# A new order for the prologue of two LoRA layers: x1, x2 and layer 1's rows loaded in front of A, three places for transposed x, and the table ends stored and gathered by themselves

## The reference

```python
# layer 0
result = jnp.einsum('bsd,od->bso', x, base_weight) + base_bias
h = jnp.einsum('bsd,brd->bsr', x, lora_A_w[ids0])
x = x + result + jnp.einsum('bsr,bor->bso', h, lora_B_w[ids0])
# layer 1
Bx = jnp.einsum('bni,bri->bnr', x, B[ids1])
x = x + jnp.einsum('bnr,bor->bno', Bx, A[ids1])   # scaling is 1
```

## Time and profile before

| | |
|---|---|
| time, median of 3 runs | 98.22 us (97.95 to 98.42) |
| the profiled execution | 97.92 us |
| its span, first to last instruction | 95.8 us |
| busy: PE, DVE, ACT, POOL | 91.5, 64.8, 58.7, 58.0 us |
| moved by DMA | 19.45 MB |
| mean granted clock of TensorE | 0.997 |

### The profile page before, as it was taken

One profiled execution on the slowest core, in us unless ns is written; L12 is line 12 of the kernel. 1 busy time (PEld: TensorE's weight loads), 2 busy tenths in 40 slices (PEclk: granted clock), 3 DMA queues, 4 the chain that ended last, 5 costly groups with the idle time before them and its releaser, 6 DMA issues.

```text
span 95.8 us, 2305 instructions
## 1 busy us (share of the span) xinstructions
PE 91.5 (96%) x662; PEld 90.0 (94%) x662; DVE 64.8 (68%) x120; ACT 58.7 (61%) x189; POOL 58.0 (61%) x126
## 2 busy tenths in 40 slices
PE   5999999999999999999999999999999999999980
PEld 5899999999899998999999999999999999999970
DVE  4499799227076468959587877768595868786460
ACT  0074598874588796748494948567584949480210
POOL 6504008850568999999576584959585766808500
PEclk9999999999999999999999999999999999999998
DMA  2999998968896289989996499992836354520205
GB/s 40 312 347 387 374 403 262 281 156 214 215 224 223 53 250 238 310 249 235 203 290 218 70 319 209 238 269 91 228 44 229 34 213 54 200 110 0 110 0 219
DMA packets 16335, 19.45 MB, mean 203 GB/s; under 512 B 1444, under 2 KB 11556, under 8 KB 16164
## 3 DMA queue, kind: packets, MB, share of 16 engines
q1 hardware_dynamic: 15040, 14.04, 50.1%
q0 software_dynamic: 1280, 5.28, 22.1%
q10 hardware_dynamic: 4, 0.00, 0.0%
HBM read 13.47 MB, written 5.84 MB: 202 GB/s over the span
## 4 chain that ended last, share of the span: by engine, by line
PE 90%; DVE 4%; ACT 2%; issue 1%; DVEq 0%; ACTq 0%
PE psum L394 55%; PE psum L440 11%; PE psum L432 4%; PE psum L362 4%; PE psum L480 4%; PE psum L378 4%; PE psum L370 3%; DVE table_rounded L640 3%; PE psum L466 2%; PE psum L414 1%; PE psum L405 1%; PE psum L448 1%; DVE y L679 1%; ACT row_ends L558 1%; ACT table_rounded L558 1%
## 5 line engine op out<-in xcount | busy, mean ns | idle before, releaser
L394 PE MATMUL psum<-wd,xt 128*128 128x256 f32 (+1 forms) x384 | 62.3, 310 | 0.0
L394 PEld LDWEIGHTS psum<-wd,xt 128*128 128x128 f32 x384 | 56.1, 188 | 0.0
L558 ACT ACTIVATE wd<-table_rounded 128x128 fp32r x128 | 27.7, 297 | 14.7 <-PE psum L394 12.5
L339 POOL TENSOR_TENSOR up_rows<-gathered_rows,up_rows 128x512 fp32r<-128x512 f32 x16 | 20.6, 1289 | 14.0 <-ACT up_rows L558 14.0
L322 POOL DMA_INDIRECT gathered_rows<-by_rank,rows x16 | 15.9, 996 | 6.3 <-DMA by_rank<-row_ends 3.8
L640 DVE TENSOR_TENSOR xt<-psum,xt 128x512 fp32r<-128x512 f32 x16 | 11.1, 691 | 6.6 <-ACT xt L558 5.9
L647 DVE STREAM_TRANSPOSE psum<-x_squares 128x512 f32<-128x512 f32 x13 | 14.4, 1110 | 0.0
L440 PE MATMUL psum<-up_rows,u_sel 128*128 128x256 f32 x96 | 14.2, 284 | 0.0
L440 PEld LDWEIGHTS psum<-up_rows,u_sel 128*128 128x128 f32 x96 | 12.8, 190 | 0.2
L659 DVE STREAM_TRANSPOSE psum<-psum 128x128 f32<-128x128 f32 x16 | 5.3, 330 | 11.2 <-PE psum L394 7.8
L332 POOL TENSOR_TENSOR g_sel<-gathered_rows,batch_mask 128x16 f32<-128x16 f32 x64 | 12.1, 227 | 0.9 <-DMA gathered_rows<-by_rank,rows 0.7
(11 more groups left out here) (60 smaller groups left out, 72.1 us busy)
## 6 DMA issues: line engine op xcount, KB each, us to landing
out<-y SPq DMA_DIRECT2D x15, 256.0 KB
x_squares<-in_x SPq DMA_DIRECT2D x8, 256.0 KB
w_rows<-in_L_cond_base_weight SPq DMA_DIRECT2D x4, 256.0 KB, 4.0
bw_rows<-in_L_cond_lora_B_w SPq DMA_DIRECT2D x1, 1024.0 KB, 7.0
a_rows<-in_L_cond_lora_A_w SPq DMA_DIRECT2D x1, 1024.0 KB, 9.2
by_rank<-bw_by_rank SPq DMA_DIRECT2D x4, 256.0 KB
x_squares<-in_x SPq DMA_DIRECT2D x8, 128.0 KB
x_rows<-in_x SPq DMA_DIRECT2D x3, 256.0 KB, 9.3
```

Of the source, the lines that this page charges most:

```text
L339: nc.gpsimd.tensor_tensor(out=up_rows[:, k % 2, LO, :], in0=gathered_rows[:, k % GATHERS, 0:D], in1=up_rows[:, k % 2, HI, :], op=ALU.subtr ...
L394: last = nc.tensor.matmul(bank_of(k, half)[:, start:end], xt[:, k % 2, c, x_part, :], wd[:, w_part, c, col:col + end - start], start=(c == ...
L558: return nc.scalar.activation(dst, src, ACT.Copy)
```

## The change

- **Loads.** SP loads x1 and x2 directly behind Bw, then A1's rows, the ids and the bias, and A last of all.
- **Start.** One warm-up product less, the two fillers gone; the copy of b1's columns moves from VectorE to ScalarE, which calls its table early.
- **xt** has three places. x2 is transposed and split before G, and base(2)'s left half is multiplied in front of D; base(0)'s right half is then one piece with D, and the separate `down` products go. up(0) stands one chunk (three products) before base(2)'s end, not two.
- **The table.** A row begins with its end (G, bias, padding: 148 numbers are stored) and is 660 numbers long instead of 644. The ends are stored in front of A1's rows, with a semaphore of their own. POOL gathers block 0's ends by themselves (a row is five units of 132 numbers), then waits for the rows; own_u(0) and g_select(0) read the small gather, and POOL issues all four gathers before g_select(1).
- **Block 0's low rows** are made on VectorE instead of POOL, and own_u(0) goes before x_turn(3). On ScalarE up_high(0) goes behind xt_high(3) and u_high(0), and a select reads its adapters before it waits.
- SP waits for gather 0 before it issues x's group 4.

```diff
--- before.py
+++ after.py
...
 SLOTS = 3
-WARM_UPS = 6
-FILLERS = 2
+X_SLOTS = 3
+WARM_UPS = 5
...
 GROUPS = (N0 + N1) * R // P
-G_COL, BB_COL = D, D + P
-ROW = BB_COL + 4
+G_COL, BB_COL = 0, P
+ENDS = P + 4
+UNITS = 5
+ROW = UNITS * ENDS
+UP_AT = ROW - D
...
 gathered_rows = sb("gathered_rows", [P, GATHERS, ROW])
-xt = sb("xt", [P, 2, C, 2, P], F32R)
+first_ends = sb("first_ends", [P, ENDS])
+xt = sb("xt", [P, X_SLOTS, C, 2, P], F32R)
...
+def ends(k, col, width):
+    if k == 0:
+        return first_ends[:, bass.ds(col, width)]
+    return gathered_rows[:, k % GATHERS, bass.ds(col, width)]
+def wait_ends(engine, k):
+    if k == 0:
+        engine.wait_ge(first_ends_gathered, 16)
+    else:
+        engine.wait_ge(gathered[k % GATHERS], 16 * (k // GATHERS) + 16)
+def wait_up_rows(engine, k):
+    if k == 0:
+        engine.wait_ge(first_up_ready, 1)
+    else:
+        engine.wait_ge(up_ready, k)
...
 def store_by_rank(queue, by_rank_part, n, row, c):
-    view = by_rank_dram[row:row + n * R, c * P:(c + 1) * P].rearrange("(n r) o -> n r o", r=R)
+    view = by_rank_dram[row:row + n * R, UP_AT + c * P:UP_AT + (c + 1) * P].rearrange("(n r) o -> n r o", r=R)
...
     sp.dma_start(bw_rows[:, :, :], lora_b.rearrange("n (c p) r -> (n c) p r", p=P)).then_inc(bw_in, 16)
-    sp.dma_start(a_rows[:, :, :], lora_a.rearrange("(g n) r d -> (n r) g d", g=C)).then_inc(a_in, 16)
     load_x(1)
+    load_x(2)
...
                  l1_a.rearrange("n (c p) r -> (n c) p r", p=P)).then_inc(a1_in, 16)
-    load_x(2)
...
     sp.dma_start(bias_all[:, :], bias.rearrange("(a n) -> a n", a=1).to_broadcast([P, D])).then_inc(bias_in, 16)
+    sp.dma_start(a_rows[:, :, :], lora_a.rearrange("(g n) r d -> (n r) g d", g=C)).then_inc(a_in, 16)
...
         store_by_rank(sp, bw_by_rank, N0, 0, c)
+    sp.wait_ge(zeros_ready, 2)
+    sp.wait_ge(bias_b1_ready, 1)
+    wait_drained(sp, "g")
+    sp.dma_start(by_rank_dram.rearrange("(g p) c -> p g c", p=P)[:, :, 0:UP_AT], row_ends[:, :, :]).then_inc(ends_stored, 16)
...
         store_by_rank(sp, a1_by_rank, N1, N0 * R, c)
-    sp.wait_ge(zeros_ready, 2)
-    sp.wait_ge(bias_b1_ready, 1)
-    wait_drained(sp, "g")
-    sp.dma_start(by_rank_dram.rearrange("(g p) c -> p g c", p=P)[:, :, D:ROW], row_ends[:, :, :]).then_inc(table_stored, 16)
...
     for k in range(NBLK - 1):
+        if k == 0:
+            sp.wait_ge(gathered[0], 16)
...
     nc.gpsimd.tensor_copy(rows[:, :], row_sums[:, :]).then_inc(rows_ready, 1)
+    nc.gpsimd.tensor_scalar(out=first_units[:, :], in0=row_sums[:, 0:1], scalar1=float(UNITS), scalar2=None,
+                            op0=ALU.mult).then_inc(rows_ready, 1)
...
         n1 = adapters_of(pool, k, L1)
-        pool.wait_ge(gathered[k % GATHERS], 16 * (k // GATHERS) + 16)
+        wait_ends(pool, k)
...
             last = nc.gpsimd.tensor_tensor(
-                out=g_sel[:, k % 2, b, L1, :], in0=gathered_rows[:, k % GATHERS, bass.ds(n1[b] * R + G_COL, R)],
+                out=g_sel[:, k % 2, b, L1, :], in0=ends(k, n1[b] * R + G_COL, R),
...
-    pool.wait_ge(rows_ready, 1)
+    pool.wait_ge(rows_ready, 2)
...
     pool.wait_ge(masks_ready, 4)
-    pool.wait_ge(table_stored, (2 * C + 1) * 16)
+    pool.wait_ge(ends_stored, 16)
+    nc.gpsimd.indirect_dma_start(out=first_ends[:, :], out_offset=None,
+                                 in_=by_rank_dram.rearrange("n (u c) -> (n u) c", c=ENDS),
+                                 in_offset=bass.IndirectOffsetOnAxis(ap=first_units[:, 0:1], axis=0),
+                                 ).then_inc(first_ends_gathered, 16)
+    pool.wait_ge(table_stored, 2 * C * 16)
...
     gather(1)
+    g_select(0)
     gather(2)
-    for k in range(NBLK):
+    gather(3)
+    for k in range(1, NBLK):
...
-    def base(k, chunks, with_d=True, halves=range(2), group_check=True):
+    def base(k, chunks, halves=range(2)):
...
-    def down(k, chunks):
-        half, at = U_AT[k % 2]
-        for c in chunks:
-            for x_part, d_part in HALVES:
-                nc.tensor.matmul(bank_of(k, half)[:, at:at + P], xt[:, k % 2, c, x_part, :],
-                                 wd[:, d_part, c, D_AT[k % 2]:D_AT[k % 2] + P],
-                                 start=False, stop=True, skip_group_check=True)
...
     w_fill(0)
-    keep_warm(FILLERS)
...
     base(0, range(C), halves=[0])
+    x_fill(2)
...
     base(1, range(C), halves=[1])
-    x_fill(2)
+    wait_x(2)
+    wait_drained(pe, "a0")
+    base(2, range(C), halves=[0])
...
     wait_drained(pe, "c1")
-    base(0, [0, 1], halves=[1], with_d=False, group_check=False)
     wait_d(0)
-    down(0, [0, 1])
-    base(0, [2, 3], halves=[1], group_check=False)
+    base(0, range(C), halves=[1])
...
-    wait_x(2)
-    base(2, range(C), halves=[0])
...
     wait_d(2)
-    base(2, [0, 1], halves=[1])
+    base(2, range(0, C - 1), halves=[1])
     up(0)
-    base(2, [2, 3], halves=[1])
+    base(2, [C - 1], halves=[1])
...
         act.wait_ge(xt_filled, k + 1)
+        if k >= X_SLOTS:
+            act.wait_ge(u_filled, k - X_SLOTS + 1)
+        copy(xt[:, k % X_SLOTS, :, HI, :], chunked(XT)).then_inc(xt_hi_ready, 1)
+    def select(k, layer, n=None):
+        ready, table = ((sel0_ready, table0_rounded), (sel1_ready, table1_rounded))[layer]
+        n = n or adapters_of(act, k, layer)
...
             act.wait_ge(u_filled, k - 1)
-        copy(xt[:, k % 2, :, HI, :], chunked(XT)).then_inc(xt_hi_ready, 1)
-    def select(k, layer, n=None):
-        ready, table = ((sel0_ready, table0_rounded), (sel1_ready, table1_rounded))[layer]
-        if k >= 2:
-            act.wait_ge(u_filled, k - 1)
-        n = n or adapters_of(act, k, layer)
...
+    act.wait_ge(warm_ready, 1)
+    copy(table_call[:, :], warm[:, 0:1])
+    wait_filled(act, "b1")
+    copy(b1_cols[:, :, :], chunked(fill_of("b1"))).then_inc(act_drained, 1)
+    w_high(0)
...
     first = {(k, layer): adapters_of(act, k, layer) for k in range(2) for layer in (L0, L1)}
-    for oc in range(C):
+    for oc in range(1, C):
...
     copy(a1_by_rank[:, 0:R // 2, :], a1_rows[:, :, 0:R // 2].rearrange("p o r -> p r o")).then_inc(a1_by_rank_ready, 1)
+    xt_high(2)
...
     select(1, L0, first[1, L0])
-    xt_high(2)
...
     select(2, L1)
-    up_high(0)
...
     u_high(0)
+    up_high(0)
...
     plus(0)
-    wait_filled(dve, "b1")
-    nc.vector.tensor_copy(b1_cols[:, :, :], chunked(fill_of("b1"))).then_inc(dve_drained, 1)
...
     xt_low(0)
-    for q in range(4):
+    def lay_bw(q):
...
+    for q in range(3):
+        lay_bw(q)
+    xt_low(1)
+    lay_bw(3)
...
     low(table1_rounded[:, :, LO, :, :], c1_by_adapter(), table1_rounded[:, :, HI, :, :]).then_inc(dve_drained, 1)
-    xt_low(1)
...
                             op0=ALU.mult).then_inc(ids_f_ready, 1)
+    xt_low(2)
...
     turn_u(0)
-    xt_low(2)
+    own_u(0)
     x_turn(3)
-    own_u(0)
...
     turn_u(1)
+    dve.wait_ge(up_hi_ready, 1)
+    low(up_rows[:, 0, LO, :], gathered_rows[:, 0, UP_AT:ROW], up_rows[:, 0, HI, :]).then_inc(first_up_ready, 1)
```

More of the change, by code:

```diff
@@ L87, in two_lora_layers @@
         rows = sb("rows", [P, NBLK], U32)
+        first_units = sb("first_units", [P, 1], U32)
         bias_b1_terms = sb("bias_b1_terms", [P, D])
         gathered_rows = sb("gathered_rows", [P, GATHERS, ROW])
-        xt = sb("xt", [P, 2, C, 2, P], F32R)
+        first_ends = sb("first_ends", [P, ENDS])
+        xt = sb("xt", [P, X_SLOTS, C, 2, P], F32R)
         up_rows = sb("up_rows", [P, 2, 2, D], F32R)
@@ L96, in two_lora_layers @@
         warm = sb("warm", [P, P])
+        table_call = sb("table_call", [P, 1])
         y = sb("y", [P, SLOTS, D])
@@ L147, in two_lora_layers @@
         up_hi_ready, up_ready = sem("up_hi_ready"), sem("up_ready")
+        first_up_ready = sem("first_up_ready")
         g_ready = sem("g_ready")
@@ L381, in c1_part @@
                     last.then_inc(filled, 1)
-            def base(k, chunks, with_d=True, halves=range(2), group_check=True):
+            def base(k, chunks, halves=range(2)):
                 left = W_LEFT[k % 2]
                 regions = [(left, left + HALF, P), (left, left + HALF, P + HALF)]
-                if with_d:
-                    at_half, at = U_AT[k % 2]
-                    start = min(at, left)
-                    regions[at_half] = (start, start + HALF + P, min(D_AT[k % 2], P + at_half * HALF))
+                at_half, at = U_AT[k % 2]
+                start = min(at, left)
+                regions[at_half] = (start, start + HALF + P, min(D_AT[k % 2], P + at_half * HALF))
                 for c in chunks:
@@ L393, in base @@
                             start, end, col = regions[half]
-                            last = nc.tensor.matmul(bank_of(k, half)[:, start:end], xt[:, k % 2, c, x_part, :],
+                            last = nc.tensor.matmul(bank_of(k, half)[:, start:end], xt[:, k % X_SLOTS, c, x_part, :],
                                                     wd[:, w_part, c, col:col + end - start],
```

(22 more changed lines are left out.)

17 lines of the change are left out of this document (9 added, 8 removed).

## The result

The changed kernel takes 102.72 us (median of 4 runs, 100.51 to 104.35) beside 98.32 us (97.95 to 98.62) for the kernel before on the same chip. The ratio is 1.028 (95% interval 1.017 to 1.039). The forecast was 97.5 with a range of 96.9 to 98.8: wrong in sign and size. Measured again (`e15`) it was 103.12 against 98.67, 1.043 (1.032 to 1.054).

The account below looks back on a forecast made before the run. TensorE, 96% busy, was taken as the bound, so add_gh(1)'s shift sets the end: up(0) at 31.25 and three base(2) products, 0.50, give 32.48 against 33.17, -0.69; hence 97.23 profiled, median 97.5, range 96.9 to 98.8.

Parts of the forecast that it names:

- Start: Kernel start: removing the 0.75 us fillers gains 0.50, as 0.25 is lost to the clock's lower level.
- To G: Stretch up to product G: G waits for the fourth bw_cols copy, starting at 16.0 instead of 16.20, 0.20 gained.
- A later ... Cost nothing: Before A's transposes: A lands at about 17, they start at 19.6; no cost below a delay of 2.6 us.
- rival 4: Loads at the start: A comes after 19.6; at 21.1 it would cost +0.8 us, 99.0; chance 0.03.
- The queue's contents are unchanged: Load queue at the start: its last load was in at 16.93 before, so A is in at about 17.
- To D: From G to D's columns: D starts at 24.4; base(0)'s right half gains 0.59; add_gh(0) can begin at 28.45 against 30.09.
- (b): Chain of the ends before up(0): store in at 23.9, small gather in at 27.05, up(0) at 31.25.
- (c): Chain of layer 1's rows before up(0): gather 0 in at 29.8, high and low half done at 31.2.
- rival 1: Before up(0): the ends, or gather 0, come late; up(0) at 32.9 means +1.0 us, 99.2; chance 0.18.
- group 4 and y(0)'s store queue behind it ... nothing: SP's wait for gather 0: no cost, as y(0) is there only at 33 and block 4's x is turned at 35.5.
- nothing changes: In the loop: no change in time, although gathered rows are 2.5% longer.
- three places for x only loosen a wait: In the loop: the third xt place costs nothing; one of the reasons for expecting no change there.

Follow-up runs that it names:

- e15: The unaltered changed kernel run again beside the kernel before, for another profile: 103.12 against 98.67, ratio 1.043.
- e8: Kernel before with only the change's start (one warm-up product and the fillers gone, b1's copy on ScalarE): 98.5 against 98.45, ratio 1.001.
- e5: Changed kernel with table part undone (layer 1's stores first, one gather, no SP wait, own_u(0) behind x_turn(3)), wider ends-first rows kept: 101.7 against 98.45.
- e11: Kernel before with only the change's load order (x1 and x2 in front, A last): 99.97 against 98.47, ratio 1.016.
- e9: e5 with A's load moved directly behind x2's: 99.49 against 98.47, ratio 1.009.
- e12: Kernel before with the change's start, and x1 and x2 loaded first with A directly behind them: 98.19 against 98.47, ratio 0.998.
- e6: Changed kernel with layer 1's stores in front of the ends' again and no SP wait, small gather kept: 101.65 against 98.45, ratio 1.029.
- e1: Changed kernel without SP's wait for gather 0 before x's group 4: 100.41 against 98.49, ratio 1.013.
- e14: Changed kernel with A behind x2, old table order, one gather, no SP wait, 644-number rows and block 0's old order: 98.88 against 98.67, ratio 1.003.
- e2: Kernel before with only SP's wait for gather 0 added: 98.48 against 98.49, ratio 0.9993.
- e10: Changed kernel with only A's load moved directly behind x2's: 101.67 against 98.47.
- e16: Kernel before with only three places for xt: 98.52 against 98.49, ratio 0.998.
- after: The first profiled run of the unaltered changed kernel: 104.35 us, span 102.2.
- e7: Kernel before with only the ends' store moved in front of layer 1's rows: 101.68 against 98.45, ratio 1.026.
- e4: Kernel before with x groups 3 and 4 loaded early, right behind the bias: 104.09 against 98.49.
- e3: Changed kernel without SP's wait, x groups 3 and 4 loaded right behind A: 105.9 against 98.49, ratio 1.073.

## Why the prediction was wrong, step by step

- **Start.** Right, the w0 transposes end and c1's first part starts at 5.67. Its eight products took 0.89 us, 111 ns each as before, so the 0.25 us set aside for the lower clock was not paid here. The gain is real and worth nothing alone (`e8`), since G waits for x1's load there.
- **To G.** G at 15.70, forecast 16.0: right, and 0.3 better. The step that failed first is "A later ... Cost nothing". I asked when A itself is needed: in this profile it landed at 18.5, and its transposes start behind G at 19.5. But that was luck: with the same order of loads it came at 19.8 in `e15`, 20.1 in `e5` and 20.2 in `e11`, and TensorE waited 0.47, 0.60 and 0.93 us for it. This is rival 4, to which I gave 0.03. The larger fault is that I did not ask what stands behind A. A megabyte now sits on the queue in front of Bw's stores and the ends, and the broadcast loads, which used to run beside A, run alone at a DMA share of 0.13 to 0.52 for 3 us. `e11` shows the price of this order, 1.6% or 1.5 us; `e5` against `e9` points the same way, with too much spread in `e5` for a figure. That the hole is the reason is read from the traces: with A in front of the broadcasts (`e12`) it is gone and the ends land in 3.43 us, with A last they took 5.01 to 5.95 (`e5`, `e6`, `e11`, `e15`), but 4.26 in the first profile and 3.22 in `e1`. "The queue's contents are unchanged" was true of bytes and false of time.
- **To D.** Right: 24.42, forecast 24.4, and base(0) in one piece. TensorE was ready for add_gh(0) at 28.8 and waited 1.10 for it. So the head start was real, and worth nothing. `e14` has it, `e12` a part of it, and both show the time of before, since with gather 0 in at 28.7 to 28.9 TensorE waits for g_sel (1.11 and 0.20 us). The prediction did count this chain for up(0), in (b) and (c); what its reading of the earlier trace rows hid is how near it was already: g_sel(0), behind gather 0, ended at 28.96 + 0.77 = 29.73 and add_gh(0) began at 30.09, 0.4 of slack.
- **Late next (b), the ends.** Store forecast in at 23.9, measured 24.44 (26.0 in `e15`, and 24.14 in `e1`, issued 0.7 later: this landing varies by more than the gain that was forecast). The 4.1 that I read from the earlier trace rows as the store's landing holds 0.81 us of POOL's start behind it; the store itself took 3.3. That start was left out behind the new landing. The lower bound of 0.7 was misread as well: the earlier trace rows gives a wait of SP, and in the changed kernel the last stores of y took 1.9 us from issue to landing. So the small gather began at 25.32 instead of 23.9. It was in at 28.05, 1.54 behind its issue's end, where I took 2.0. The estimate after the Trainium skill (DMA: Bandwidth & Descriptors, Anatomy of one DMA) was 2.15; counted from there the trace is below it, and counted from the issue's begin (2.7) above.
- **(c), the rows.** Gather 0 in at 30.47 (32.11 in `e15`), forecast 29.8: the small gather costs 1.5 us of POOL in front of it, and both terms above it slipped. up(0) at 32.01 instead of 31.25. By itself that is a loss of 0.6, rival 1 in its mild form.
- **(c), "group 4 and y(0)'s store queue behind it ... nothing".** This is the step that ended last, with up(2) 3.6 us late in both profiles; 2.60 us of idle time belong to it in the first and 0.53 in `e15`, where the late ends had already cost 3.5. I gave x 5.7 us between gather 0 and its use (29.8 to 35.5), and never asked for a price of its landing. It was issued from 30.48 to 32.2, beside gathers 1 to 3, and took 6.9 to 8.7 us. `e2` shows that the wait is free with gather 0 at 29.0, `e10` that up(2) is already 1.2 late (39.54) with gather 0 in at 29.35, `e1` that without it gather 0 suffers instead. That the gathers beside it slow the loads is only a guess from the traces; neither that nor POOL's earlier gather 3 was tried alone.
- **In the loop "nothing changes".** Wrong by 0.05 to 0.06 us in each block: from the up at 48.63 to the last add_gh the lateness grows from 5.83 to 6.35, by 0.5; "three places for x only loosen a wait" held (`e16`), so the reason given was right and the verdict not.
- **Not in any rival.** A wait in which TensorE stands idle for about 2 us can also cost clock: 0.50 for about 3 us behind it (`after`, `e1`, `e5`, `e7`, `e15`). In `after` up(2) was 3.64 late and the second up behind it 5.83, 2.2 us more, of which 0.2 is idle time; in `e7` the span is 3.6 longer against 2.5 at up(0), 1.1. Rival 1's price of 1.0 us left this out, so the range ended at 98.8.

No version that was run beats the kernel before by more than can be measured; the best, `e12` and `e16`, stand at 0.998.

## What to carry to other kernels

When a load is moved back on a queue, cost what is queued behind it, not only its own arrival; and look at the queue's share while slow loads run alone. Where a chain of waits is one engine throughout, find the second chain's slack before crediting a head start. A wait in front of loads must be costed with a landing time read under the traffic of that place, and an idle time of TensorE of some 2 us with the clock that it may lose.

## What the hardware showed that was not expected

- While the two ids broadcasts and the bias broadcast load with nothing large beside them, the DMA share is 0.13 to 0.52 for about 3 us (0.04 to 0.45 in `e15`). Before, with A ahead of them, the share was 1.0 there.
- The landing of the same ends' store varied widely: 592 bytes a row took 2.98 us (`e10`), 3.22 (`e1`), 4.26 (`after`), 4.53 (`e9`) and 5.95 (`e15`); 528 bytes took 3.3 (before) to 5.51 (`e4`).
- POOL spends 0.80 to 0.82 us between the last store's landing and its first indirect DMA (every chain that passes there), and 0.30 in front of the next one.
- With more loads in front of them on the queue SP's issues themselves took longer: Bw's four stores 6.12 us in `e4` instead of 2.71, the ends' store 0.82 in `e3` instead of 0.38.
- The granted clock fell to 0.50 behind 1.77 us (`e5`) to 2.6 us (`after`) of idle TensorE and stayed there for about 3 us. Behind 1.94 us in `e9` it stayed at 1.00, as it did behind 1.1 us (add_gh(0) of `after` and `e14`), so the length of the idle time alone does not say which level follows.
- Products of 384 columns took 341 to 342 ns on average in the loop in one family of kernels and 337 in the other, with the same weight loads (188 to 189 ns).
